# One attention and mixture-of-experts layer: stack copies split over two DMA queues, buffer padding moved, and two engine orders changed

## The chip, the core and the metric

The program runs on one core of one Trainium2 chip. The time is the device time of one execution in microseconds (us). "Engine" means TensorE (PE, the matrix products), VectorE (DVE), ScalarE (ACT), GpSimd (POOL) and SyncE (SP, which here only starts DMA transfers). Each engine runs its own list of instructions strictly in order and waits on semaphores. A wait or a DMA issue that stands in the list holds up everything behind it on that engine.

## What is computed

Sixteen sequences of 128 tokens with 128 features go through one layer. Cut to what matters:

```python
q, k, v = norm(x) @ Wq.T + bq, ctx @ Wk.T + bk, ctx @ Wv.T + bv   # 16 heads of 8 features
s = q @ k.T / sqrt(8) + m[h] * softplus(1000 + |i - j|)           # per head, a slope m[h]
x = x + softmax(s) @ v @ Wo.T + bo
h = norm(x)
c = the two largest of softmax(h @ Wr), zero elsewhere            # 16 experts
x = x + sum_e c[e] * (silu(h @ Wg[e]) * (h @ Wu[e])) @ Wd[e] + shared expert
```

## The kernel before, in words

The 16 sequences are taken as 8 groups of two (`b` is 0 or 1). The work is a software pipeline: `step(f, a, p, q, abuf)` does the feed-forward part of group `f`, the attention of group `a = f + 1`, the query and key projection of group `p = a + 1` and the first normalisation of group `q = p + 1`. Every engine has its own `step`, written out by hand, and that text is the order of its instructions. The calls are: some lines of prologue, `step(None, 0, 1, 2, 0)` (below: step 0), `step(0, 1, 2, 3, 1)` (step 1), a loop of four steps (steps 2 to 5), `step(5, 6, 7, None, 0)` (step 6), `step(6, 7, None, None, 1)` (step 7), and a last stage that does the feed-forward part of group 7.

**Stacks.** The scores need about float32 accuracy, so each query and key value is split into a high and a low float16 part, made by ACT (`qk_high`, L613) and DVE (`qk_low`, L798) in the four slots `t` of `qk_parts`. Four DMAs per group (`stacks`, L211, one for each slot, 128 KB each, 128 partitions to 8) lay them head by head into rows 8t to 8t+7 of `stacks_sb`, which has two buffers. The score products (`scores`, L324 and L327; `scores_T`, L360 to L370) contract over 96 or 98 rows of it. Rows 32 to 95 are never written by the copies and must be zero, and rows 96 and 97 of the key stacks must be one: these are the **pads**. Before, DVE and POOL write them for buffer 0 in the prologue (L1023, L1028, L1034, L1165) and POOL writes those of buffer 1 after step 0 (L1176, L1178, L1180).

**Shift rows.** DVE takes the negated row maxima of the scores (`row_max`, L818), splits them (`max_high`, `max_low`, L824 and L828), PE transposes them (`shift_T`, L336), ACT copies them to `nmT` (L620) and starts a small DMA of 8 KB (`shift_rows`, L630) into rows 96 and 97 of the query stacks. `scores_T(a, b, 0)` waits for that DMA. ACT has had one queue for these, for the router weights (L634) and for some weight loads; SP has had the queue of all else.

**Experts.** PE computes chunk `c` of the hidden layer (`up`, L446 and L451; 9 chunks), ACT takes tanh (L671), DVE multiplies (`gate`, L923; `hidden`, L929). POOL multiplies chunks 0 to 7 in pairs by the router weights (`weigh_experts`, L1139), which were spread by a DMA to `crep` (L218). PE then does `down` (L472) for the chunks, one step late, among the next step's work. In the last stage of the program the weights are spread on PE (`spread`, L564 and L565) and DVE multiplies (`weigh_chunk`, L1043). POOL also computes the inverse deviations (`inverse_deviation2`, L1107 and L1111), which DVE's second normalisation (`norm2`, L870) waits for, and PE's `expert_in_T` (L415) waits for that.

`keep_clock` (L271) issues transposes whose results nobody reads, so that PE has work.

## Time and profile before

| | us |
|---|---|
| median of 3 runs | 289.34 (288.31 to 290.44) |
| the profiled execution | 289.88 |
| span of the profile in it | 288.1 |
| PE busy | 231.9 |
| DVE busy | 185.9 |
| ACT busy | 107.3 |
| POOL busy | 80.9 |

The profile is one execution. Its span leaves out 1.8 us around the instructions. Idle time costs something only where the waiting engine is on the path that sets the end; PE's gaps are therefore what to look for here, and then what each gap waited for.

### The profile page before, as it was taken

The numbers are of one execution on the slowest core, as the hardware profiler recorded it, in microseconds if no ns is written. First come the engines' busy times: TensorE is split into PE (matmuls) and PEld (weight loads), VectorE is DVE, ScalarE is ACT, GpSimd is POOL, SyncE is SP. The second block draws the span as 40 slices with busy tenths as digits, with TensorE's granted clock in tenths as the row PEclk, the third lists the DMA queues.
The fourth block names the chain that finished last, engine by engine and source line by source line (L and its number), as shares of the span: only waits on it lengthen the run. The fifth ranks groups of instructions, "written<-read, shape, count | busy, mean of one in ns | idle before, by whom it ended". The sixth has DMA issues, their size and how long they took to land.

```text
span 288.1 us, 5914 instructions
## 1 busy us (share of the span) xinstructions
PE 231.9 (80%) x1953; PEld 186.5 (65%) x1953; DVE 185.9 (65%) x641; ACT 107.3 (37%) x255; POOL 80.9 (28%) x124
## 2 busy tenths in 40 slices
PE   3634788129887999799979997999799969995896
PEld 3523645027655986688668776877687758765785
DVE  4751823218928883898489758975895587543664
ACT  1151344003462356244614561455235512651320
POOL 3520001793004600451055106410730071017000
PEclk9995578857999999999999999999999988997999
DMA  4244238000450044214511470137023600070000
GB/s 141 83 55 100 45 60 284 0 2 19 57 134 17 23 56 109 59 24 56 135 33 24 54 161 3 37 41 160 4 47 34 167 0 5 3 167 0 0 20 18
DMA packets 16022, 17.54 MB, mean 61 GB/s; under 512 B 1920, under 2 KB 14704, under 8 KB 16000
## 3 DMA queue, kind: packets, MB, share of 16 engines
q1 hardware_dynamic: 14800, 15.83, 25.9%
q10 hardware_dynamic: 1200, 1.43, 1.7%
q8 instruction: 12, 0.20, 0.3%
q14 instruction: 10, 0.08, 0.1%
HBM read 11.77 MB, written 1.16 MB: 45 GB/s over the span
## 4 chain that ended last, share of the span: by engine, by line
PE 39%; issue 27%; POOL 14%; DMA 10%; DVE 5%; ACT 2%; POOLq 1%; SPq 0%; ACTq 0%; DVEq 0%
PE ps_m L472 8%; PE ps_up L446 6%; DMA stacks_sb<-nmT 6%; POOL hid L1139 5%; PE ps_pv L389 4%; PE ps_s L327 3%; PE ps_st L360 3%; DMA stacks_sb<-qk_parts 3%; PE ps_up L451 2%; POOL rstd L1111 2%; PE ps_st L370 2%; PE ps_pv L396 2%; DVE xn L790 1%; PE ps_up L271 1%; DMA x_all<-in_x 1%
## 5 line engine op out<-in xcount | busy, mean ns | idle before, releaser
L472 PE MATMUL ps_m<-wd_sb,hid 128*128 128x128 f32 x288 | 47.2, 294 | 13.3 <-POOL hid L1139 13.3
L818 DVE TENSOR_REDUCE nmax<-ps_s 128x4 f32<-128x512 f32 x64 | 43.4, 682 | 20.7 <-PE ps_s L327 19.8
L923 DVE SCALAR_TENSOR_TENSOR tg<-th,ps_up 128x256 f32<-128x256 f32 x72 | 29.9, 416 | 33.6 <-ACT th L671 33.3
L472 PEld LDWEIGHTS ps_m<-wd_sb,hid 128*128 128x128 f32 x288 | 38.9, 199 | 15.9 <-issue 8.0
L626 ACT ACTIVATE probs<-ps_st 128x512 f32<-128x512 f32 x64 | 38.0, 597 | 29.9 <-PE ps_st L370 25.4
L671 ACT ACTIVATE th<-ps_up 128x256 f32<-128x256 f32 x72 | 27.6, 384 | 35.6 <-PE ps_up L451 35.6
L1139 POOL TENSOR_TENSOR hid<-hid,crep 128x512 f32<-128x512 f32 x28 | 34.7, 1269 | 0.0
L1107 POOL TENSOR_TENSOR ve<-mv,eps_sb 128x1 f32<-128x1 f32 x16 | 3.0, 190 | 96.8 <-DVE mv L863 96.8
L929 DVE TENSOR_TENSOR hid<-tg,ps_up 128x256 f32<-128x256 f32 x72 | 29.6, 411 | 0.7
L327 PE MATMUL ps_s<-stacks_sb 96*128 96x128 f16 x256 | 26.5, 240 | 1.9 <-DVE nmax L818 1.9
L446 PE MATMUL ps_up<-x_hi,wg_hi 128*128 128x256 f32 x72 | 26.9, 374 | 0.5 <-ACT x_hi L652 0.5
L370 PE MATMUL ps_st<-stacks_sb 98*128 98x128 f16 x256 | 25.0, 221 | 0.9 <-ACT probs L626 0.9
L1099 POOL TENSOR_TENSOR ve<-mv,eps_sb 128x2 f32<-128x2 f32 x8 | 1.5, 193 | 85.2 <-DVE mv L782 85.2
L327 PEld LDWEIGHTS ps_s<-stacks_sb 96*128 96x128 f16 x256 | 19.8, 108 | 7.8 <-DVE nmax L818 3.5
L370 PEld LDWEIGHTS ps_st<-stacks_sb 98*128 98x128 f16 x256 | 18.6, 98 | 8.1 <-issue 1.1
L324 PE MATMUL ps_s<-slope_hi,dist 128*128 128x512 f16 x16 | 7.1, 442 | 18.7 <-POOL stacks_sb L1180 10.9
L652 ACT ACTIVATE x_hi<-ps_st 128x256 fp32r<-128x256 f32 x8 | 3.1, 383 | 51.0 <-PE ps_st L415 51.0
L446 PE MATMUL ps_up<-x_hi,wg_lo 128*128 128x256 f32 x72 | 20.4, 284 | 0.0
L446 PE MATMUL ps_up<-x_hi,wu_lo 128*128 128x256 f32 x72 | 20.4, 283 | 0.0
L446 PE MATMUL ps_up<-x_hi,wu_hi 128*128 128x256 f32 x72 | 20.4, 283 | 0.0
L451 PE MATMUL ps_up<-x_lo,wg_hi 128*128 128x256 f32 x72 | 20.4, 283 | 0.0
L451 PE MATMUL ps_up<-x_lo,wu_hi 128*128 128x256 f32 x72 | 20.2, 280 | 0.0
(126 smaller groups left out, 486.2 us busy)
## 6 DMA issues: line engine op xcount, KB each, us to landing
crep<-cw_dram SPq DMA_DIRECT2D x14, 512.0 KB, 6.5
stacks_sb<-qk_parts SPq DMA_DIRECT2D x32, 128.0 KB
out_y<-x_all SPq DMA_DIRECT2D x8, 128.0 KB, 6.3
wg_sb<-in_wgT ACTq DMA_DIRECT2D x1, 576.0 KB, 3.3
wu_sb<-in_wuT ACTq DMA_DIRECT2D x1, 576.0 KB, 3.3
wd_sb<-in_wd SPq DMA_DIRECT2D x1, 576.0 KB, 5.8
x_all<-in_x SPq DMA_DIRECT2D x2, 256.0 KB, 3.4
ctx_all<-in_ctxT SPq DMA_DIRECT2D x2, 256.0 KB, 4.0
```

The costliest lines, as they stand in the source:

```text
L327: last = mm(bank[:, o:o + P], qs[buf][0:ZROWS, h, b * P:(b + 1) * P], ks[buf][0:ZROWS, h, b * P:(b + 1) * P], start=(g > 0), stop=True, sk ...
L370: last = mm(bank[:, o:o + P], ks[buf][:, h, b * P:(b + 1) * P], qs[buf][:, h, b * P:(b + 1) * P], start=first, stop=True, skip_group_check ...
L389: last = mm(ps_pv[32 * c:32 * c + 32, r * 3 * P:(r * 3 + n) * P], v_aug[:, b, r, c, :], probs[:, b, h * P:(h + n) * P], start=True, stop=T ...
L446: mm(ps_up[c % 2][:, k, :], w[:, c, :], x2_hi[:], start=(k == 0 and n == 0), stop=False, skip_group_check=True)
L451: last = mm(ps_up[c % 2][:, k, :], hi[:, c, :], x2_lo[:], start=False, stop=True, skip_group_check=True)
L472: last = mm(ps_dn[:, b * P:(b + 1) * P], hid[:, buf, c, b * P:(b + 1) * P], wd_sb[:, c, :], start=(c == 0 and b == 0), stop=(c == SHARED), ...
L626: fn(probs[:, b, g * HG * P:(g + 1) * HG * P], ps_st[g % 2][:], ACT.Exp).then_inc(exp_sb, 1)
L671: fn(th[:, c % 2, :], ps_up[c % 2][:, 0, :], ACT.Tanh, scale=0.5).then_inc(tanh_sb, 1)
L818: v.tensor_reduce(nmax[:, b, HG * g:HG * g + HG], ps_s[g % 2][:].rearrange("p (h j) -> p h j", h=HG), AX_X, ALU.max, negate=True).then_inc ...
L923: v.scalar_tensor_tensor(out=tg[:, c % 2, :], in0=th[:, c % 2, :], scalar=1.0, in1=ps_up[c % 2][:, 0, :], op0=ALU.add, op1=ALU.mult).then_ ...
L929: v.tensor_tensor(hid[:, buf, c, :], tg[:, c % 2, :], ps_up[c % 2][:, 1, :], ALU.mult).then_inc(hid_sb, 1)
L1139: g.tensor_tensor(h2, h2, c2, ALU.mult).then_inc(hc_sb, 1)
```

## The change

- **Pads.** DVE zeroes all 98 rows of half of buffer 0, ACT the other half and the ones of buffer 0, both at the start. ACT writes zeros and ones of buffer 1 in the prologue, after its slope tables. POOL writes no pads.
- **Prologue on DVE.** The scaling of the query weights stands ahead of the first normalisation.
- **Query and key parts.** On ACT `qk_high` comes ahead of `x2_high`; on DVE the two `qk_low` come between the first three `row_max` of a step.
- **Stack slots.** Slots 0 and 1 are issued by SP, slots 2 and 3 by ACT (`mixed_stacks`), behind `tanh(f, 1)` and ahead of the copy and the DMA of the first shift rows.
- **POOL.** Pair 0 of the experts of group `f` is weighed at the end of step `f`, between the two inverse deviations, in place of the start of the next.
- **Last stage.** `expert_in_T` comes behind two `down` chunks in place of four, the other `down` of group 6 follow, and all `down` of group 7 come at the end. The DVE order is adapted.

```diff
@@ sync
-                for t in range(4):
+                for t in range(2):
                     if t == 1:
                         sp.wait_ge(qklo_sb, 2 * p + 2)
                     sp.dma_start(stacks_sb[DH * t:DH * (t + 1), buf]..., qk_parts[:, t]...).then_inc(s_stack, 16)
@@ scalar
+            def mixed_stacks(p, buf):
+                if not (at_start(p) or (isinstance(p, int) and p == 1)):
+                    act.wait_ge(st_mm, 2 * NHG * (p - 1))
+                if at_start(p):
+                    act.wait_ge(dve_pads, 1)
+                elif isinstance(p, int) and p == 1:
+                    act.wait_ge(act_pads, 3)
+                act.wait_ge(qklo_sb, 2 * p + 2)
+                for t in range(2, 4):
+                    act.dma_start(stacks_sb[DH * t:DH * (t + 1), buf]..., qk_parts[:, t]...).then_inc(s_stack, 16)
+                if ps: qk_high(p)
                 if fs: x2_high(f)
-                if ps: qk_high(p)
                 if fs:
                     tanh(f, 0)
                     tanh(f, 1)
+                if ps: mixed_stacks(p, 1 - abuf)
...
+            act.wait_ge(zero_sb, 2)
+            fill(stacks_sb[:, 0, H // 2:], zero)
+            act.wait_ge(act_pads, 1)
+            act.wait_ge(dve_pads, 1)
+            fill(ks[0][ZROWS:AROWS], ones16)
             x_T(0)
...
             qk_high(0)
+            mixed_stacks(0, 0)
...
+            fill(stacks_sb[:, 1], zero)
+            act.wait_ge(act_pads, 3)
+            fill(ks[1][ZROWS:AROWS], ones16)
             act.wait_ge(s_stack, 64)
             act.dma_start(wu_sb[:], wuT).then_inc(s_wu, 16)
@@ vector
                     row_max(a, 0, 1)
-                    row_max(a, 0, 2)
+                if ps: qk_low(p, 0)
+                if as_: row_max(a, 0, 2)
+                if ps: qk_low(p, 1)
@@ gpsimd
-                    for pair in range(PAIRS):
+                    for pair in range(1, PAIRS):
                         weigh_experts(f - 1, pair, abuf)
...
                     inverse_deviation2(a, 0)
+                    if f is not None:
+                        weigh_experts(f, 0, 1 - abuf)
                     inverse_deviation2(a, 1)
...
-            g.memset(stacks_sb[SROWS:2 * SROWS, 1].bitcast(F32), 0.0).then_inc(second_pads, 1)
-            g.memset(stacks_sb[2 * SROWS:ZROWS, 1].bitcast(F32), 0.0).then_inc(second_pads, 1)
-            g.memset(ks[1][ZROWS:AROWS].bitcast(F32), two_ones).then_inc(second_pads, 1)
@@ tensor, last stage
-            down(f - 1, (0, 1, 2, 3), 1 - last, f)
+            down(f - 1, (0, 1), 1 - last, f)
             expert_in_T(f)
+            down(f - 1, (2,), 1 - last)
...
-            down(f, range(2, NCH), last, weighted_sb=hw_sb)
+            down(f, range(NCH), last, weighted_sb=hw_sb)
```

ACT at the start of step 1, before. L604 is the transposed input, L652 the high part of the experts' input, L613 the high parts of queries and keys, L671 tanh, L620 and L630 the shift rows' copy and DMA:

```order
L604 ACTIVATE xnT<-ps_st 128x256
L652 ACTIVATE x_hi<-ps_st 128x256
L613 ACTIVATE qk_parts<-ps_st,bqk_sb 128x2x256 x2
L671 ACTIVATE th<-ps_up 128x256 x2
L620 ACTIVATE nmT<-ps_pv 32x128
L630 DMA stacks_sb<-nmT 2x16x128
L671 ACTIVATE th<-ps_up 128x256
```

The same place with the change (L653 is a stack slot, L620 and L627 stand for the parts of queries and keys and for the shift rows' copy, L637 for their DMA):

```order
L611 ACTIVATE xnT<-ps_st 128x256
L620 ACTIVATE qk_parts<-ps_st,bqk_sb 128x2x256 x2
L672 ACTIVATE x_hi<-ps_st 128x256
L691 ACTIVATE th<-ps_up 128x256 x2
L653 DMA stacks_sb<-qk_parts 8x16x512 x2
L627 ACTIVATE nmT<-ps_pv 32x128
L637 DMA stacks_sb<-nmT 2x16x128
L691 ACTIVATE th<-ps_up 128x256
```

The two stack slots now stand between tanh and the shift rows, and the parts come ahead of the experts' input.

DVE at the start of step 1, before (L870 is norm2, L877 the low part of the experts' input, L798 the low parts of queries and keys):

```order
L870 TENSOR_SCALAR x2n<-x_all,mv,rstd 128x128
L818 TENSOR_REDUCE nmax<-ps_s 128x4 x2
L877 TENSOR_TENSOR x_lo<-ps_st,x_hi 128x256
L818 TENSOR_REDUCE nmax<-ps_s 128x4
L824 CAST nsplit<-nmax 128x16
L923 SCALAR_TENSOR_TENSOR tg<-th,ps_up 128x256
L828 TENSOR_TENSOR nsplit<-nmax,nsplit 128x16
L929 TENSOR_TENSOR hid<-tg,ps_up 128x256
L798 SCALAR_TENSOR_TENSOR qk_parts<-ps_st,bqk_sb,qk_parts 128x2x256
L818 TENSOR_REDUCE nmax<-ps_s 128x4
L798 SCALAR_TENSOR_TENSOR qk_parts<-ps_st,bqk_sb,qk_parts 128x2x256
```

The same place with the change:

```order
L904 TENSOR_SCALAR x2n<-x_all,mv,rstd 128x128
L852 TENSOR_REDUCE nmax<-ps_s 128x4
L832 SCALAR_TENSOR_TENSOR qk_parts<-ps_st,bqk_sb,qk_parts 128x2x256
L852 TENSOR_REDUCE nmax<-ps_s 128x4
L832 SCALAR_TENSOR_TENSOR qk_parts<-ps_st,bqk_sb,qk_parts 128x2x256
L911 TENSOR_TENSOR x_lo<-ps_st,x_hi 128x256
L852 TENSOR_REDUCE nmax<-ps_s 128x4
L858 CAST nsplit<-nmax 128x16
L957 SCALAR_TENSOR_TENSOR tg<-th,ps_up 128x256
L862 TENSOR_TENSOR nsplit<-nmax,nsplit 128x16
L963 TENSOR_TENSOR hid<-tg,ps_up 128x256
```

The two low parts moved from behind the first `hidden` to ahead of the experts' low part.

POOL in the second half of step 1, before (L1099 and L1103 are the inverse deviations of the first normalisation, L1107 and L1111 those of the second):

```order
L1132 COPY ctx_g<-ctx_all 128x256
L1099 TENSOR_TENSOR ve<-mv,eps_sb 128x2
L1103 TENSOR_TENSOR rstd<-ve,neg_half 128x2
L1107 TENSOR_TENSOR ve<-mv,eps_sb 128x1
L1111 TENSOR_TENSOR rstd<-ve,neg_half 128x1
L1107 TENSOR_TENSOR ve<-mv,eps_sb 128x1
L1111 TENSOR_TENSOR rstd<-ve,neg_half 128x1
```

The same place with the change:

```order
L1168 COPY ctx_g<-ctx_all 128x256
L1135 TENSOR_TENSOR ve<-mv,eps_sb 128x2
L1139 TENSOR_TENSOR rstd<-ve,neg_half 128x2
L1143 TENSOR_TENSOR ve<-mv,eps_sb 128x1
L1147 TENSOR_TENSOR rstd<-ve,neg_half 128x1
L1175 TENSOR_TENSOR hid<-hid,crep 128x512
L1143 TENSOR_TENSOR ve<-mv,eps_sb 128x1
L1147 TENSOR_TENSOR rstd<-ve,neg_half 128x1
```

One pair's multiply (L1175) now stands between the two inverse deviations of the second normalisation.

## Rows read from the trace of the kernel before

**Rows 1.** Waits, longest first: engine, line, what released it: us, times, longest.

```profile
PE ps_m L472 <- POOL hid L1139: 13.3, 7, 3.1
...
PE ps_s L324 <- POOL stacks_sb L1180: 10.9, 1, 10.9
```

**Rows 2.** Timeline 0 to 38: start, us, engine, line, operation, count, idle before, releaser.

```profile
6.29 3.68 DVE L790 TENSOR_SCALAR xn<-x_all,mv,rstd 128x128 f32<-128x128 f32 x2 [1.16 <-POOL rstd L1103]
6.31 3.50 POOL L1165 MEMSET stacks_sb<- 32x4096 f32 x1
...
14.66 3.38 SPq L211 DMA_DIRECT2D stacks_sb<-qk_parts  x4
...
25.59 0.61 PE L324 MATMUL ps_s<-slope_hi,dist 128*128 128x512 f16 x1 [7.42 <-DMA stacks_sb<-qk_parts]
...
28.90 1.26 ACT L613 ACTIVATE qk_parts<-ps_st,bqk_sb 128x512 f16<-128x512 f32 x2 [1.69 <-PE ps_st L293]
...
37.00 0.63 PE L360 MATMUL ps_st<-slope_hi,dist 128*128 128x512 f16 x1
```

**Rows 3.** A group by form on ACT: busy us, mean ns of one, idle before.

```profile
L739 ACT ACTIVATE wg_hi<-wg_sb 128x1152 fp32r<-128x1152 f32 x1 | 1.2, 1163 | 6.3 <-DMA stacks_sb<-qk_parts 6.3
```

**Rows 4.** Timeline of step 0, second shift rows on ACT, and SP's next transfer behind them.

```profile
39.06 0.63 ACTq L630 DMA_DIRECT2D stacks_sb<-nmT  x1
...
41.22 0.34 SPq L227 DMA_DIRECT2D x_all<-in_x  x1
```

**Rows 5.** Timeline of PE in step 4, a step of the loop.

```profile
149.95 0.71 PE L472 MATMUL ps_m<-wd_sb,hid 128*128 128x128 f32 x4 [1.39 <-POOL hid L1139]
...
159.27 0.38 PE L360 MATMUL ps_st<-slope_hi,dist 128*128 128x512 f16 x1
...
160.63 0.23 PE L336 MATMUL ps_pv<-ident,nsplit 128*32 128x128 f16 x1
...
165.31 0.38 PE L360 MATMUL ps_st<-slope_hi,dist 128*128 128x512 f16 x1 [0.40 <-DMA stacks_sb<-nmT]
```

**Rows 6.** Timeline of DVE in the same step.

```profile
149.06 0.92 DVE L870 TENSOR_SCALAR x2n<-x_all,mv,rstd 128x128 f32 x1
...
152.24 0.42 DVE L877 TENSOR_TENSOR x_lo<-ps_st,x_hi 128x256 fp32r<-128x256 f32 x1 [0.62 <-ACT x_hi L652]
...
155.97 0.73 DVE L798 SCALAR_TENSOR_TENSOR qk_parts<-ps_st,bqk_sb,qk_parts 128x512 f16<-128x512 f32 x1
...
174.49 0.34 DVE L870 TENSOR_SCALAR x2n<-x_all,mv,rstd 128x128 f32 x1 [0.19 <-POOL rstd L1111]
```

**Rows 7.** Timeline of ACT and SP in the same step (q: the engine's DMA issues).

```profile
154.48 0.38 ACT L671 ACTIVATE th<-ps_up 128x256 f32<-128x256 f32 x1 [0.84 <-PE ps_up L451]
...
155.25 0.67 ACTq L630 DMA_DIRECT2D stacks_sb<-nmT  x1
...
161.19 0.63 ACTq L630 DMA_DIRECT2D stacks_sb<-nmT  x1
...
153.29 5.42 SPq L211 DMA_DIRECT2D stacks_sb<-qk_parts  x4
```

**Rows 8.** Busy time by microsecond, same step: last columns clock, DMA share, GB/s.

```profile
158.00:159.00 1.00, 1.00 (x10) 0.98 (x9) 1.00 (x4) 0.12 (x1) 0.00 (x0) 1.00 0.51 126
159.00:160.00 1.00, 1.00 (x11) 0.75 (x11) 0.97 (x3) 0.42 (x2) 0.00 (x0) 1.00 0.57 54
...
163.00:164.00 1.00, 1.00 (x15) 0.95 (x12) 0.74 (x5) 0.82 (x2) 0.08 (x1) 1.00 0.36 29
```

**Rows 9.** Timeline of PE, starts of step 7 and of the last stage.

```profile
234.34 0.68 PE L472 MATMUL ps_m<-wd_sb,hid 128*128 128x128 f32 x4 [2.48 <-POOL hid L1139]
...
262.84 3.47 PE L472 MATMUL ps_m<-wd_sb,hid 128*128 128x128 f32 x16 [3.15 <-POOL hid L1139]
```

**Rows 10.** Timeline of DVE at the start of the last stage and the end.

```profile
261.51 1.27 DVE L870 TENSOR_SCALAR x2n<-x_all,mv,rstd 128x128 f32<-128x128 f32 x1 [0.63 <-POOL rstd L1111]
...
285.30 0.42 DVE L934 TENSOR_TENSOR x_all<-ps_m,x_all 128x256 f32<-128x256 f32 x1 [1.29 <-PE ps_m L472]
```

More of the change, by code:

```diff
@@ L314, in scores @@
                         pe.wait_ge(act_setup, 1)
-                        pe.wait_ge(own, 8)
-                        pe.wait_ge(stack_pads, 2)
+                        pe.wait_ge(own, 7)
+                        pe.wait_ge(dve_pads, 1)
+                        pe.wait_ge(act_pads, 1)
                     elif isinstance(a, int) and a == 1:
-                        pe.wait_ge(second_pads, 3)
+                        pe.wait_ge(act_pads, 4)
                 elif b == 0 and g == 1:
@@ L572, in _ @@
             up(f, 1)
+            down(f - 1, (3,), 1 - last)
+            up(f, 2)
             down(f - 1, (4,), 1 - last)
-            up(f, 2)
+            up(f, 3)
             down(f - 1, (5,), 1 - last)
-            up(f, 3)
+            up(f, 4)
             down(f - 1, (6,), 1 - last)
             weights_T(f, None)
-            up(f, 4)
+            up(f, 5)
             down(f - 1, (7,), 1 - last)
@@ L584, in _ @@
             spread(0, 1)
-            up(f, 5)
+            up(f, 6)
             down(f - 1, (8,), 1 - last)
             spread(2, 3)
-            up(f, 6)
+            up(f, 7)
             spread(4, 5)
-            down(f, (0,), last, weighted_sb=hw_sb)
-            up(f, 7)
+            up(f, 8)
             spread(6, 7)
-            down(f, (1,), last, weighted_sb=hw_sb)
-            up(f, 8)
-            down(f, range(2, NCH), last, weighted_sb=hw_sb)
+            down(f, range(NCH), last, weighted_sb=hw_sb)
         @block.scalar
@@ L717, in step, with fill @@
                 if fs: tanh(f, 8)
+            def fill(tile, column):
+                words = tile.bitcast(F32)
+                fn(words, bass.AP(column, 0, [[1, words.shape[0]]] + [[0, n] for n in words.shape[1:]]), ACT.Copy).then_inc(act_pads, 1)
             nc.scalar.preload_act_table(ACT.Exp)
-            act.wait_ge(s_x, 16)
+            act.wait_ge(zero_sb, 2)
[3 more added lines that the diff above has]
+            fill(ks[0][ZROWS:AROWS], ones16)
             x_T(0)
@@ L751, in _ @@
             tanh(f, 3)
+            tanh(f, 4)
             act.wait_ge(cwT_mm, f + 1)
             fn(cwT_hi[:], ps_cwT, ACT.Copy).then_inc(cwT_sb, 1)
-            for c in range(4, NCH):
+            for c in range(5, NCH):
                 tanh(f, c)
@@ L959, in step @@
                 if fs: hidden(f, 0, 1 - abuf)
-                if ps: qk_low(p, 0)
                 if as_: row_max(a, 1, 0)
-                if ps: qk_low(p, 1)
                 if fs: gate(f, 1)
@@ L1020, in step @@
                     norm2_mean(a, 1)
-            v.memset(stacks_sb[2 * SROWS:ZROWS, 0, 0:H // 2].bitcast(F32), 0.0).then_inc(stack_pads, 1)
-            step(None, None, None, 0, 0)
+            v.memset(zero[:], 0.0).then_inc(zero_sb, 1)
+            v.memset(ones16[:], two_ones).then_inc(zero_sb, 1)
+            v.memset(stacks_sb[:, 0, 0:H // 2].bitcast(F32), 0.0).then_inc(dve_pads, 1)
+            norm1_stats(0)
+            norm1_mean(0)
             dve.wait_ge(s_wqkvo, 32)
@@ L1027, in _ @@
             v.tensor_scalar(bqk_sb[:, 0:1], bqk_sb[:, 0:1], q_scale, None, ALU.mult).then_inc(dve_setup, 1)
-            v.memset(stacks_sb[2 * SROWS:ZROWS, 0, H // 2:].bitcast(F32), 0.0).then_inc(stack_pads, 1)
+            norm1(0)
             norm1_stats(1)
@@ L1033, in _ @@
             norm1(1)
-            v.memset(ks[0][ZROWS:AROWS].bitcast(F32), two_ones).then_inc(stack_pads, 1)
             values(0)
@@ L1045, in _ @@
             gate(f - 1, 8)
+            hidden(f - 1, 8, 1 - last)
             norm2(f, 1)
-            hidden(f - 1, 8, 1 - last)
             x2_low(f)
@@ L1064, in _ @@
             hidden(f, 3, last)
+            gate(f, 4)
+            hidden(f, 4, last)
             dve.wait_ge(cwT_sb, f + 1)
             v.tensor_tensor(cwT_lo[:], ps_cwT, cwT_hi[:].bitcast(F32), ALU.subtract).then_inc(cwTlo_sb, 1)
-            gate(f, 4)
-            hidden(f, 4, last)
+            gate(f, 5)
+            hidden(f, 5, last)
             weigh_chunk(0)
-            gate(f, 5)
-            residual2(f - 1)
-            hidden(f, 5, last)
             weigh_chunk(1)
             gate(f, 6)
+            residual2(f - 1)
+            hidden(f, 6, last)
             weigh_chunk(2)
-            hidden(f, 6, last)
             weigh_chunk(3)
             gate(f, 7)
+            hidden(f, 7, last)
             weigh_chunk(4)
-            hidden(f, 7, last)
             weigh_chunk(5)
             gate(f, 8)
+            hidden(f, 8, last)
             weigh_chunk(6)
-            hidden(f, 8, last)
             weigh_chunk(7)
@@ L1164, in _ @@
             pool.wait_ge(rstd1_sb, 1)
-            g.memset(stacks_sb[SROWS:2 * SROWS, 0].bitcast(F32), 0.0).then_inc(own, 1)
-            pool.wait_ge(own, 7)
             copy_ctx(0)
@@ L1185, in _ @@
             run_steps(pool, step)
-            for pair in range(PAIRS):
+            for pair in range(1, PAIRS):
                 weigh_experts(NG - 2, pair, (NG - 2) % 2)
```

19 lines of the change are left out of this document (12 added, 7 removed).

## The prediction

> **What bounds the kernel now.** I read the list of waits first, because a long wait of PE points at a place. Two stand out. PE waited once for 10.9 us for POOL's pads of buffer 1, and 7 times, 13.3 us in all, for POOL's first expert pair [rows 1]. The timeline of the prologue shows why the start is slow: two normalisation multiplies took 3.68 us together while POOL's 3.50 us memset ran beside them, and the first stacks came 10.93 us after SP began to issue them (14.66 to 25.59) [rows 2]. In a loop step PE's own rows tell how much of the 13.3 us is to be had. PE waited 1.39 us for POOL at 149.95, then had work nearly without a gap to the first `scores_T` at 159.27, the second `shift_T` at 160.63 and `scores_T` of the second sequence at 165.31, which waited 0.40 us for the second shift rows [rows 5]. But DVE in the same stretch had a gap of only 0.62 us [rows 6], and PE follows DVE's row maxima there. So DVE is the near bound of the first half of a step, and at most some 0.6 us of the 1.39 us can come back by moving POOL alone. At the starts of step 7 and of the last stage PE waits 2.48 and 3.15 us [rows 9].
>
> **Part 1, pads and prologue.** POOL's three memsets leave, so PE's wait of 10.9 us goes [rows 1]. What is late next is not POOL: PE had been done with step 0 at 51.9 (62.81 less 10.91), and the normalisation chain of step 0 was finished some 1.5 us later, for which PE has 1.5 us of scores and projections to do first. I take 10.9 us.
>
> DVE's multiplies, without the memset beside them, should take 0.7 instead of 3.68 us: one such multiply took 0.34 us beside an idle POOL [rows 6]. PE's warm-up transposes end at 7.2, so PE starts about 2.8 us earlier. The stacks are then issued from 11.8 and 13.3 instead of 14.66 and 16.1. With all four slots served as before they are complete 9.5 us after the second of these, at 22.8, against 25.59.
>
> Against this stand ACT's fills. 1152 elements took 1163 ns [rows 3], so 4096 take 3.6 to 4.1 us and 2048 about 1.9 us. The first two (3.9 us) lie in ACT's idle time before 10 us and cost nothing. The pair of buffer 1 (5.5 us) stands behind the slope tables, which end near 18.9, so ACT is busy until 24.4, and with the 1.4 us of weight copies behind it until 26. `qk_high` of group 1 began at 28.90 before [rows 2], and can now begin at 26.1 at the earliest, even if the stacks are there sooner. `qk_low` now stands ahead of DVE's third row maximum, so step 0 hangs on this. Adding DVE's own times puts the end of its row maxima at 33.0 (34.9 before) and PE's `scores_T` at 35.2 by engines alone, against 37.00 before [rows 2]: 1.8 us earlier. The first shift rows, however, now stand in ACT's queue behind slots 2 and 3, which are issued from 29.5. They land at 35.6 if the two queues run side by side, at 37.8 if slots 1 to 3 share one rate. So step 0 moves by between -1.4 and +0.8 us. I take -0.4, between them. Prologue and step 0 together: -10.9 - 0.4 = **-11.3 us** (-10.1 to -12.7). Step 1 has fewer PE chunks and waited 1.38 us for its second shift rows; there the loss of part 2 and this wait cancel.
>
> **Part 2, slots 2 and 3 on ACT.** This is the part that can cost. First the speed of a slot. A slot that is alone moves its 128 KB in one microsecond (126 GB/s). Slots 2 and 3, queued behind it, move at 54 GB/s and are at it until about 163.6 [rows 8], so each takes 2.25 us. The share of busy DMA time is about a half in either case. From issue (156.8 for slot 1) a first slot is done after 2.2 us, a second after 4.45 us. Shift rows: the second ones were issued at 161.19, while slots were moving, and PE got them at 165.31, 4.1 us later [rows 5, 7]. In step 0 a set issued at 39.06 had landed when SP went on at 41.22, 2.15 us later [rows 4].
>
> With the change, in the times of that step: ACT's `tanh(f, 1)` is dispatched at about 154.7 (154.48 before [rows 7], PE being 0.2 us later, as below). Each slot then takes the queue 0.65 us to issue, as SP's four took 5.42 us with a wait inside [rows 7]; the copy of the shift rows comes 1.3 us later, and their DMA is issued at 156.35 in place of 155.25. In the same queue it stands behind two slots that are complete 4.45 us after 154.75, at 159.2. It moves after them and lands 1.1 to 1.6 us after its data, near 160.9. PE needed it at 159.27 [rows 5]. It had 4.0 us of cover before, and has none now.
>
> What comes back: the second shift rows no longer meet moving slots and land in some 2.2 us, so the 0.40 us wait goes [rows 5], and DVE, ahead while PE stands, no longer holds `shift_T` back, 0.25 us. Net: 1.6 - 0.65 = +0.95 us in a step. The steps that have both a stack and a full load are 2 to 6, five of them.
>
> The Trainium skill bears on this twice. Its page "DMA: Bandwidth & Descriptors" says under "Why a DMA increments its semaphore by 16 and not by 1" that a DMA uses as many engines as divide the slowest dimension of both sides, from the lowest number up: 8 for a slot with 8 destination partitions, 2 for the shift rows, so these two share rings. The half share in the rows agrees. Under "Issuing engines are not separate DMA queues" it says that issuing from several engines saves only the issue time. That speaks against splitting; by it step 0 is 1.2 us worse than I took.
>
> **Part 3, POOL order and DVE parts.** Down chunk 0 no longer waits for POOL. In a loop step PE spends that time waiting elsewhere: `qk_low` twice (0.7 us each [rows 6]) now stands ahead of the experts' low part, which moves from 152.24 to about 152.9, so PE ends its first `up` chunk 0.4 us later than before, and the DVE gap of 0.62 us closes. By the first `scores_T` PE would be only 0.2 us ahead, and part 2 takes that. New at the end of a step is POOL's 1.26 us multiply beside DVE. A DVE multiply took 0.92 us at 149.06 beside POOL and 0.34 us at 174.49 without [rows 6]; about 0.25 us of this gets onto the chain to the next row maximum. It needs `crep`, whose data ended near 173.0 in this step, to have landed by 174.45; it probably has. So +0.15 to +0.25 us in a step, and part 2 and 3 together are **+1.1 us in each of five steps, +5.5 us**. Bounds for one step: -0.2, if the slots on ACT go at the rate of lone ones (shift rows land at 159.5), and +2.8, if they hold the shift rows until 162.5.
>
> **Part 4, step 7 and last stage.** No stacks are copied here. In step 7 PE's 2.48 us wait goes [rows 9]; what is late next is `norm2`, which ends at 234.3, against a transpose at 235.6 before, and from 236 to 239 the granted clock was 0.5 (1.2 GHz), after the idle time. I take -2.2 (between -1.0, with the clock as before, and -3.0). In the last stage `expert_in_T` need not wait for four pairs, only for `norm2` at 262.8 (261.51 + 1.27 [rows 10]) in place of 266.1. PE's work is the same in sum and saturates PE from 273 on; its end at 285.30 [rows 10] comes earlier by the idle time saved, 3.3 us less one `down` chunk (0.45) and less what a low clock costs again. I take -2.5 (-1.5 to -3). Together **-4.7 us**.
>
> **Sum.** 289.88 for the profiled execution - 11.3 + 5.5 - 4.7 = 279.4. It was 0.5 us above the median of the three runs, so by the median 278.9, rounded to 279.
>
> **Rivals.** (A) The shift rows keep their cover: slots on ACT go like lone ones or the small DMA is served between them. For: PE's trace shows a first slot done in one microsecond of data. Against: the second of a pair never did. -0.2 in a step gives 289.3 - 11.3 - 1.0 - 4.7 = 272.3. (B) The shift rows wait longer, +2.8 in a step: 289.3 - 11.3 + 14 - 4.7 = 287.3; half way, 283.5. For: the 4.1 us of the set that met the slots in another queue; a shared queue can only be harder. (C) Slower than before: the same wait, from the point where it costs 3.2 us net in a step, that is where the shift rows land at 163 or later, 6.7 us after their issue, because each slot on ACT then takes above 3.2 us. At +4 us in a step it is 289.3 - 16.0 + 20 = 293.3. Against: no slot took more than 2.3 us. (D) POOL's moved pair waits for `crep` and holds up the second inverse deviation, as POOL does nothing behind a waiting instruction. If it lands 1 us later than I read, 0.7 us in six steps is added: 283. (E) The pads' gain is not had, because ACT's fills hold step 0: with `qk_high` 3 us later than I took, 282.
>
> **How the numbers follow.** Forecast, 276 to 282: 0.50. (A), 270 to 276: 0.22. (B), (D) and (E), 282 to 286.4: 0.14. Within 1%, 286.4 to 292.2, about what a measurement here can tell from no change (the upper end of B): 0.07. (C) and worse: 0.07. Range 270.5 to 286.4, which leaves out some 0.15, and it takes in both ends of parts 1 and 2. Faster 0.86, same 0.07, slower 0.07.
>
> **What would show each step.** Part 1: no PE wait for POOL near 50; the first normalisation multiplies near 0.7 us; `scores_T` of step 0 at 35 to 38. Part 2: a PE wait of 1 to 2 us for the shift rows' DMA ahead of the first `scores_T` of every loop step, and none ahead of the second sequence's. Part 3: PE's wait for the first expert pair gone, a loop step of 29.3 us in place of 28.25. Part 4: a shorter wait for POOL and a first `up` of the last stage 3 us sooner in its stage. The prediction is wrong if the loop step is not longer than before, or if it is longer than 31 us.

## The result, and the profile after

The changed kernel took **295.82 us** (median; 293.68 to 296.28) against 288.82 us (287.98 to 290.44) for the kernel before: ratio 1.022, 95% interval 1.015 to 1.029. It is slower by 2.2%, where I had forecast 279. Its profiled execution took 296.10 us with a span of 294.3 us; the one of before took 289.88 us. The ratios leave out executions in a slower state that any kernel can fall into, so a ratio can differ from that of the medians beside it (most in the experiment with 281.26 us, whose profiled execution was also in that state).

The start of each step, read from PE's first scores in both timelines, splits the difference of 6.2 us between the two profiled executions:

| stretch | before, us | after, us | difference | predicted |
|---|---|---|---|---|
| up to the scores of step 1 | 62.81 | 51.05 | -11.8 | -11.3 |
| step 1 | 27.46 | 33.28 | +5.8 | 0 |
| steps 2 to 6 | 28.08, 28.46, 28.04, 28.28, 27.90 | 31.97, 31.76, 30.33, 30.38, 30.35 | +14.0 | +5.5 |
| step 7 and last stage, to the end of the span | 57.07 | 55.18 | -1.9 | -4.7 |

So the start gained what was forecast, and the steps gave back more than all of it. The list of waits of the changed kernel, longest first (engine, line, what released it: us, times, longest):

```profile
PE ps_st L367 <- DMA stacks_sb<-nmT: 13.7, 7, 2.9
PE ps_st L422 <- DVE x2n L904: 8.3, 8, 3.2
...
PE ps_s L334 <- DVE nmax L852: 5.2, 13, 0.6
PE ps_up L458 <- DVE x_lo L911: 4.6, 6, 0.9
```

The waits for POOL of [rows 1] are gone, both of them. First now is the wait of `scores_T` for the shift rows; before it was 3.1 us in 5 waits, all for the rows of the second sequence. Step 4 shows where it comes from. PE's timeline (start, us, operation, idle time ahead and what ended it), beside [rows 5]:

```profile
148.06 0.39 PE L331 MATMUL ps_s<-slope_hi,dist 128*128 128x512 f16 x1
...
149.65 0.61 PE L479 MATMUL ps_m<-wd_sb,hid 128*128 128x128 f32 x4
...
154.97 0.38 PE L458 MATMUL ps_up<-x_lo,wg_hi 128*128 128x256 f32 x1 [0.88 <-DVE x_lo L911]
...
163.29 0.39 PE L367 MATMUL ps_st<-slope_hi,dist 128*128 128x512 f16 x1 [2.02 <-DMA stacks_sb<-nmT]
...
178.39 0.38 PE L331 MATMUL ps_s<-slope_hi,dist 128*128 128x512 f16 x1
```

From the step's first scores to the first `scores_T` it took 15.23 us, against 12.46 before (146.81 to 159.27), and from there to the next step 15.10 against 15.58. All of this step's loss lies ahead of `scores_T`. DVE in the same stretch, beside [rows 6]:

```profile
147.50 1.28 DVE L904 TENSOR_SCALAR x2n<-x_all,mv,rstd 128x128 f32 x1 [0.19 <-POOL rstd L1147]
...
152.59 0.73 DVE L832 SCALAR_TENSOR_TENSOR qk_parts<-ps_st,bqk_sb,qk_parts 128x512 f16<-128x512 f32 x1
...
153.85 0.73 DVE L832 SCALAR_TENSOR_TENSOR qk_parts<-ps_st,bqk_sb,qk_parts 128x512 f16<-128x512 f32 x1
154.51 0.41 DVE L911 TENSOR_TENSOR x_lo<-ps_st,x_hi 128x256 fp32r<-128x256 f32 x1
```

and ACT, beside [rows 7]:

```profile
156.73 0.38 ACT L691 ACTIVATE th<-ps_up 128x256 f32<-128x256 f32 x1 [0.84 <-PE ps_up L458]
156.89 1.38 ACTq L653 DMA_DIRECT2D stacks_sb<-qk_parts  x2
158.46 0.27 ACT L627 ACTIVATE nmT<-ps_pv 32x128 f16<-32x128 f16 x1 [1.35 <-issue]
158.76 0.68 ACTq L637 DMA_DIRECT2D stacks_sb<-nmT  x1
```

The shift rows are issued 10.70 us into the step, 8.44 before. Of these 2.26 us, 1.35 us is ACT issuing the two slots; the rest came from DVE, where `norm2` (L904) took 1.28 us beside POOL's moved pair and `x_lo` (L911) stands behind both `qk_low` (L832). From their issue to `scores_T` the rows then took 4.5 us, as forecast. Before, PE came to `scores_T` 4.0 us after the issue and found the rows there.

Step 1 lost most. DVE, POOL and PE at its start, three rows of the changed kernel's timeline:

```profile
53.03 3.26 DVE L904 TENSOR_SCALAR x2n<-x_all,mv,rstd 128x128 f32<-128x128 f32 x1 [0.37 <-POOL rstd L1147]
53.09 3.13 POOL L1213 TENSOR_SCALAR wd_sb<-wd_sb 128x1152 f32<-128x1152 f32 x1
56.35 0.69 PE L422 MATMUL ps_st<-ident,x2n 128*128 128x128 f32 x2 [3.23 <-DVE x2n L904]
```

POOL's scaling of `wd`, which stood behind its pads before, now runs beside `norm2` of group 0, and PE waits 3.23 us. Of busy time and clock (the last three columns are granted clock, DMA share and GB/s) the next 11 us show:

```profile
57.00:68.00 11.00, 10.50 (x53) 8.77 (x50) 8.07 (x22) 2.11 (x7) 0.65 (x3) 0.50 0.23 37
```

PE is busy but at half clock, 1.2 GHz.

### The profile page after: what moved, and what is told of

The parts are those of the page before. It is cut to its first block, busy times and chain, and to the rows that moved or that the text cites. A ratio compares the mean times of both kernels' runs of the same rounds, so it can differ in the third digit from the quotient of the medians.

```text
span 294.3 us, 5927 instructions
## 1 busy us (share of the span) xinstructions
PE 238.4 (81%) x1953; PEld 191.0 (65%) x1953; DVE 184.2 (63%) x641; ACT 116.5 (40%) x259; POOL 68.7 (23%) x120
## 4 chain that ended last, share of the span: by engine, by line
PE 42%; issue 21%; DMA 11%; ACT 8%; DVE 7%; POOL 6%; ACTq 4%; POOLq 0%; DVEq 0%; SPq 0%
DMA stacks_sb<-nmT 10%; PE ps_up L453 7%; PE ps_m L479 5%; PE ps_st L367 5%; PE ps_pv L396 4%; PE ps_up L458 4%; POOL hid L1175 4%; PE ps_st L377 4%; ACTq L653 3%; DVE nmax L852 2%; ACT qk_parts L620 2%; PE ps_pv L403 2%; DVE qk_parts L832 2%; PE ps_m L416 2%; ACT probs L633 1%
## 5 line engine op out<-in xcount | busy, mean ns | idle before, releaser
L852 DVE TENSOR_REDUCE nmax<-ps_s 128x4 f32<-128x512 f32 x64 | 43.3, 681 | 10.5 <-PE ps_s L334 9.9
L1175 POOL TENSOR_TENSOR hid<-hid,crep 128x512 f32<-128x512 f32 x28 | 35.0, 1271 | 0.5 <-DMA crep<-cw_dram 0.5
L453 PE MATMUL ps_up<-x_hi,wg_hi 128*128 128x256 f32 x72 | 27.9, 388 | 0.0
L377 PE MATMUL ps_st<-stacks_sb 98*128 98x128 f16 x256 | 26.9, 232 | 0.0
L377 PEld LDWEIGHTS ps_st<-stacks_sb 98*128 98x128 f16 x256 | 20.4, 106 | 8.5 <-issue 3.2
L458 PE MATMUL ps_up<-x_lo,wg_hi 128*128 128x256 f32 x72 | 21.8, 302 | 4.6 <-DVE x_lo L911 4.6
L367 PE MATMUL ps_st<-slope_hi,dist 128*128 128x512 f16 (+1 forms) x32 | 13.1, 409 | 13.9 <-DMA stacks_sb<-nmT 13.7
L904 DVE TENSOR_SCALAR x2n<-x_all,mv,rstd 128x128 f32<-128x128 f32 (+1 forms) x16 | 20.1, 1255 | 2.4 <-POOL rstd L1147 2.0
L453 PE MATMUL ps_up<-x_hi,wg_lo 128*128 128x256 f32 x72 | 21.2, 295 | 0.0
L453 PE MATMUL ps_up<-x_hi,wu_hi 128*128 128x256 f32 x72 | 21.1, 293 | 0.0
L453 PE MATMUL ps_up<-x_hi,wu_lo 128*128 128x256 f32 x72 | 21.1, 293 | 0.0
L458 PE MATMUL ps_up<-x_lo,wu_hi 128*128 128x256 f32 x72 | 21.0, 292 | 0.0
```

Of the source, the lines that this page charges most:

```text
L367: mm(bank[:, 0:n_split * P], dist16[:], part[:, h0:h0 + n_split, :], start=first, stop=False, skip_group_check=True)
L377: last = mm(bank[:, o:o + P], ks[buf][:, h, b * P:(b + 1) * P], qs[buf][:, h, b * P:(b + 1) * P], start=first, stop=True, skip_group_check ...
L453: mm(ps_up[c % 2][:, k, :], w[:, c, :], x2_hi[:], start=(k == 0 and n == 0), stop=False, skip_group_check=True)
L458: last = mm(ps_up[c % 2][:, k, :], hi[:, c, :], x2_lo[:], start=False, stop=True, skip_group_check=True)
L852: v.tensor_reduce(nmax[:, b, HG * g:HG * g + HG], ps_s[g % 2][:].rearrange("p (h j) -> p h j", h=HG), AX_X, ALU.max, negate=True).then_inc ...
L1175: g.tensor_tensor(h2, h2, c2, ALU.mult).then_inc(hc_sb, 1)
```

## Experiments

Each edit is against the changed kernel unless another is named. The intervals are those of the ratio to the kernel before, measured on the same chip. Three theories stood at first: (1) the slots on ACT's queue hold up the shift rows; (2) the loss is made on DVE; (3) step 1 loses by the scaling of `wd`.

**All slots back on SyncE.**

```
SP:  -for t in range(2):      +for t in range(4):
ACT: -if ps: mixed_stacks(p, 1 - abuf)
```

> The changed kernel with slots 2 and 3 back behind slots 0 and 1 on SyncE's queue; everything else of the change stays. Theory 1 (the two slot issues on ScalarE, 1.38 us ahead of the shift rows, and the slots' place ahead of the rows in ScalarE's queue, are the main loss): in each of steps 2 to 6 the shift rows are issued about 1.3 us earlier, the time from the first scores to scores_T(a,0), 15.2 us in step 4 of the changed kernel, falls to about 13.3, the wait of 2.0 us there is gone, and the time is 284 to 288 us. Theory 2 (the loss is made on VectorE at the step's start, by POOL's multiply beside norm2 and by qk_low ahead of x_lo, and the wait for the rows only hides it): the rows' wait shrinks but others take its place, 15.2 falls to 14.7 at most, and the time is 292 to 295 us.

293.77 us, ratio 1.019 (1.014 to 1.024): the same as the changed kernel within the intervals, and the time that theory 2 expected. My first theory fell in this form. The rows of step 4 (its first scores are at 145.22) say why:

```profile
151.21 1.98 SPq L217 DMA_DIRECT2D stacks_sb<-qk_parts  x3
...
154.11 0.66 ACTq L637 DMA_DIRECT2D stacks_sb<-nmT  x1
...
159.67 0.54 PE L367 MATMUL ps_st<-slope_hi,dist 128*128 128x512 f16 x1 [1.79 <-DMA stacks_sb<-nmT]
```

The same kernel by microseconds (granted clock, DMA share and GB/s last):

```profile
156.00:157.00 1.00, 1.00 (x12) 0.99 (x12) 0.58 (x3) 0.50 (x2) 0.00 (x0) 1.00 0.53 53
157.00:158.00 1.00, 0.88 (x8) 0.68 (x6) 1.00 (x4) 0.38 (x1) 0.00 (x0) 1.00 0.57 66
158.00:159.00 1.00, 0.00 (x0) 0.00 (x0) 1.00 (x10) 0.00 (x0) 0.00 (x0) 1.00 0.08 5
```

The rows are issued 8.9 us into the step (9.5 on the mean of steps 2 to 6; 10.7 in the changed kernel, 8.5 before), but take 5.56 us to PE instead of the changed kernel's 4.5. What ACT saved by not issuing slots, 1.2 us, went again in the longer transfer: `scores_T` starts 15.2 us into these steps on the mean, 15.3 in the changed kernel. Nothing stands ahead of them on their own queue. Ahead of them on the other queue are slots 1, 2 and 3, since the early `qk_low` releases these at 151.21; their bytes move until about 158.1, and PE has the rows 1.6 us after that. In the changed kernel the same reading gives 1.3 us (traffic at a share of 0.40 up to 162, 0.01 behind it, `scores_T` at 163.29). So the rows reach PE 1.3 to 1.6 us after the last byte of the slots issued ahead of them, on whichever queue. Theory 1 was restated so: what counts is the slot bytes issued ahead of the rows.

**Shift rows first, two queues kept.**

```
ACT:  shift_rows(a, 0, abuf)
     +if ps: mixed_stacks(p, 1 - abuf)     (was ahead of shift_copy)
```

> The changed kernel with mixed_stacks moved behind shift_rows(a, 0) on ScalarE: still two queues, but the shift rows of the first block go ahead of the two slots. Theory 1 in its narrow form (it is the order on ScalarE alone): as good as the kernel with all slots on SyncE, 284 to 288 us, since the slots are wanted only in the next step. Rival (any slot traffic on a second queue slows the rows, whatever the order): the rows still take over 4 us from issue to scores_T and the time stays at 290 us or more. Theory 2: 292 to 295 us.

281.26 us, ratio 0.967 (0.961 to 0.973), 15.9 us less than the changed kernel by the ratios, and better than the 284 to 288 expected. No wait for the rows is left in the list of waits; in step 4 they went at 145.97, slots 2 and 3 at 146.85, and `scores_T` started without a wait at 149.57. Slots that follow 0.9 us behind, then, do not delay the rows as slots ahead of them do. The edit also takes ACT's two slot issues (1.34 us) out of the rows' way.

```profile
145.97 0.70 ACTq L637 DMA_DIRECT2D stacks_sb<-nmT  x1
146.85 1.34 ACTq L653 DMA_DIRECT2D stacks_sb<-qk_parts  x2
```

**Pair 0 back at the step's start.**

```
POOL: -for pair in range(1, PAIRS):   +for pair in range(PAIRS):
      -if f is not None: weigh_experts(f, 0, 1 - abuf)
```

> The changed kernel with POOL's pair 0 back at the start of the next step; slots stay on two queues. Theory 2: norm2(a,0) goes back from 1.28 to about 0.34 us, the rows are issued 0.5 us earlier in each step and the time is 292 us or less. Theory 1: the rows still wait for the two slots, so at most 0.5 us per step comes back, and down(0)'s wait for POOL (1.4 us in step 4 of the kernel before, 2.5 and 3.2 us in step 7 and the last stage) returns: 295 to 299 us.

297.66 us, ratio 1.030 (1.023 to 1.036). In step 4 `norm2` of block 0 is back at 0.35 us, `down` waits 1.30 us for POOL again, and the wait for the rows is 2.04 us as in the changed kernel. This is within the 295 to 299 us that theory 1 expected; the intervals of the two kernels overlap. On the mean of steps 2 to 6 the rows were issued 0.45 us earlier than in the changed kernel, which is about half of DVE's share of the delay there, and `scores_T` came 0.5 us earlier. What this gained was lost behind `scores_T`: in four of these steps the granted clock averaged 0.90 there (in two of the changed kernel's), and the one step at full clock took 29.90 us against 30.38.

**Pads and prologue alone** (the kernel before with this part of the change).

> The kernel before with only the pads and the prologue's order of the change (slots all on SyncE, loop steps and last stage as before). The sum as predicted for this part: 277 to 279 us (11 us below the kernel before). Theory 3 (part of this gain is lost again in step 1, where norm2 now runs beside POOL's scaling of wd, 3.26 us against 1.50, and TensorE's clock falls to half after the wait of 3.23 us for x2n): step 1 takes about 31 us instead of 27.5 and the time is 281 to 285 us.

276.55 us, ratio 0.960 (0.955 to 0.964): 11.8 us gained by the medians, 13.8 between the two profiled executions. The first scores of step 1 came at 46.53, 16.3 us earlier than before and 4.5 earlier than in the changed kernel, whose step 0 is 4.4 us longer (29.3 against 24.9). Step 1 took 29.1 us here, not 27.5, so 1.7 us of the gain is lost there, less than theory 3 said; the rest of the 5.8 us needs the other parts.

**qk_low late again, all slots on SyncE.** Beside the edit of the first experiment:

```
DVE:  row_max(a, 0, 1)
     -if ps: qk_low(p, 0)
      row_max(a, 0, 2)
     -if ps: qk_low(p, 1)
      ...
      hidden(f, 0, 1 - abuf)
     +if ps: qk_low(p, 0)
      row_max(a, 1, 0)
     +if ps: qk_low(p, 1)
```

> The changed kernel with all slots on SyncE and with qk_low back at its late place on VectorE (behind hidden(f,0)); pads, pair 0, qk_high first and last stage stay changed. Theory 1, as it stands after the first four runs (the shift rows wait for the bytes of all slots that were issued ahead of them, on either queue; qk_low's early place puts slots 1 to 3 ahead): slots 1 to 3 fall behind the rows again, the waits of 1.9 us for the rows in steps 2 to 6 are gone, x_lo comes 0.9 us earlier, and the time is 272 to 278 us, 16 to 21 below the kernel with all slots on SyncE and qk_low early (293.8). Rival (a slow row transfer has to do with ScalarE's issue or with the multiply beside norm2, not with qk_low's place): 288 us or more.

272.62 us, ratio 0.943 (0.939 to 0.948). This is at the low end of what theory 1 expected. With all slots on SyncE the place of two instructions of 0.73 us on DVE is worth 21 us. Step 4 (first scores 132.34) beside the first experiment: the rows go 8.3 us into it, and `scores_T` starts at 144.56 without a wait, 12.2 us into it.

```profile
135.50 8.49 SPq L217 DMA_DIRECT2D stacks_sb<-qk_parts  x4
...
140.65 0.67 ACTq L637 DMA_DIRECT2D stacks_sb<-nmT  x1
```

```profile
142.00:143.00 1.00, 1.00 (x10) 0.83 (x9) 1.00 (x3) 0.38 (x1) 0.00 (x0) 1.00 0.03 6
143.00:144.00 1.00, 1.00 (x10) 0.90 (x10) 1.00 (x5) 0.00 (x0) 0.00 (x0) 1.00 0.32 72
```

SP holds four slots in 8.49 us because it waits for `qk_low` behind slot 0. By microseconds (DMA share and GB/s at the end of the row) almost nothing moves from 138 to 143, and the rows pass ahead of slots 1 to 3.

**All slots behind the landed first rows.** The kernel of the first experiment with one wait more:

```
SP: +if not at_start(p): sp.wait_ge(s_nm[0], 16 * p)
```

> The changed kernel with all slots on SyncE and one more wait there: the slots of the next group are issued only when the first block's shift rows of this group have landed; qk_low stays early. Theory 1: no slot byte is ahead of the rows, they need 2 to 2.5 us from issue, no wait for them is left and the time is at or below the kernel that issues the rows ahead of slots 2 and 3 (281.3): 277 to 281 us. Rival (slots 0 and 1 must go early or they are late for the next step): a wait for stacks at the step's start, above 283 us.

317.70 us, ratio 1.100 (1.095 to 1.105), far from what I expected. I had thought of the first rows alone. In step 4 they are free, but the second ones are now behind all four slots:

```profile
168.83 2.73 SPq L219 DMA_DIRECT2D stacks_sb<-qk_parts  x4
...
172.20 0.63 ACTq L639 DMA_DIRECT2D stacks_sb<-nmT  x1
...
179.63 0.38 PE L369 MATMUL ps_st<-slope_hi,dist 128*128 128x512 f16 x1 [3.74 <-DMA stacks_sb<-nmT]
```

7.4 us from issue to PE with four slots ahead, 5.6 with three (SyncE alone), 4.5 with two (the changed kernel): the miss is the clearest reading of the same rule. Counted are the slots ahead whose bytes had still to move when the rows were issued.

**The rest of the change, cut up.** One kernel keeps pads, pair 0 and last stage (slots on SyncE, `qk_low` late, `qk_high` behind `x2_high`); the other keeps pads and pair 0.

> The changed kernel without its part on the stack and the q/k parts: slots all on SyncE, qk_low late, qk_high behind x2_high; it keeps pads, pair 0 on POOL at the step's end, and the last stage. Against pads alone (276.6) theory 1 has nothing for or against pair 0; from the rows of the changed kernel: no down waits for POOL any more (13.3 us in 7 waits before), x2n waits 0.3 to 0.6 us in each step, the last stage saves about 2 us: 271 to 275 us. Theory 2 (the multiply beside norm2 costs about what the waits for POOL gave): 275 to 278 us.

> Pads and pair 0 of the change alone; last stage, slots and q/k parts as in the kernel before. Tells pair 0 (against pads alone, 276.6) from the last stage (against the kernel that has it as well). Pair 0 predicted by the waits it removes in steps 2 to 7: 0 to 0.6 us a step, so 273 to 277 us; if norm2 beside the multiply costs more than the waits gave, 277 to 280 us. The last stage is predicted at 2 to 2.5 us by my term.

273.16 us (ratio 0.943, 0.939 to 0.947) and 276.81 us (0.955, 0.948 to 0.961), both as expected. Against pads alone (0.960) pair 0 moves nothing that these intervals tell; the last stage brings 3.4 us by the ratios, give or take 2, and `qk_high` first, which the kernel with 272.62 us has as well, nothing. At the start of the last stage PE waited for

```profile
248.36 3.75 PE L479 MATMUL ps_m<-wd_sb,hid 128*128 128x128 f32 x16 [3.15 <-POOL hid L1159]
```

```profile
247.82 0.69 PE L422 MATMUL ps_st<-ident,x2n 128*128 128x128 f32 x2 [1.60 <-DVE x2n L889]
```

the first with pads alone, the second with pads, pair 0 and last stage: the wait of 3.15 us for POOL became one of 1.60 us for `norm2`.

**qk_low late, two queues, rows first.** The second experiment with the DVE edit of the fifth.

> The changed kernel with qk_low late and with slots 2 and 3 on ScalarE behind the first shift rows: two queues, and no slot but slot 0 ahead of the rows. Against all slots on SyncE with qk_low late (272.6) it tells what the second queue does by itself: theory 1 says nothing for the first rows; the two slots, waiting for the late qk_low, hold ScalarE about 1.4 us plus up to 2 us ahead of tanh(2) and sit ahead of the second rows: 273 to 279 us. Rival (the second queue helps, as the change intends): under 272 us.

272.64 us, ratio 0.942 (0.935 to 0.948), equal to all slots on SyncE and between what the two expectations gave. The second queue by itself does nothing that can be told, for or against. The second experiment, which differs only in `qk_low`'s place, is 7.4 us slower by the ratios. In its list of waits 4.6 us in 6 waits for `x_lo` stand, and none here. But the steps of the two profiled executions (282.41 and 273.17 us) show most of the difference where TensorE's clock was low. In brackets is the mean granted clock ahead of the first `scores_T` and behind it:

| step | `qk_low` early, us | `qk_low` late, us |
|---|---|---|
| 1 | 31.28 (0.66, 0.92) | 29.27 (0.87, 1.00) |
| 2 | 28.25 (1.00, 1.00) | 27.94 (1.00, 1.00) |
| 3 | 29.93 (0.88, 1.00) | 28.31 (1.00, 1.00) |
| 4 | 27.82 (1.00, 1.00) | 27.42 (1.00, 1.00) |
| 5 | 28.29 (1.00, 1.00) | 28.06 (1.00, 1.00) |
| 6 | 32.57 (0.71, 1.00) | 28.62 (0.88, 1.00) |

At full clock, DVE's own share of the loss is 0.2 to 0.4 us in a step once the rows are out of it; such steps are as short as the kernel's before (27.90 to 28.46). The lower clock is not that one execution's alone: the two executions on which the ratio rests averaged 0.92 and 0.93, the four with the late `qk_low` 0.95 to 0.96. Whether the early `qk_low` brings it on was not tested.

**The kernel before with qk_low early and nothing else.**

> The kernel before with one edit: qk_low at its early place on VectorE (behind row_max(a,0,1) and row_max(a,0,2)). Theory 1: slots 1 to 3 are issued ahead of the first shift rows, the rows take 5.5 us instead of 4.0 from issue, and each of steps 1 to 6 becomes 2 to 4 us longer, as between the changed kernels with qk_low early and late (21 us): 300 to 312 us. Rival (it needs the multiply beside norm2 as well, or the waits for POOL in this kernel cover it): 290 to 296 us.

322.14 us, ratio 1.110 (1.102 to 1.117), more than I expected. A third price comes in here. ACT still makes `qk_high` behind `x2_high`, so DVE stands at the early `qk_low` and `x_lo` behind it is late:

```profile
171.07 0.75 DVE L798 SCALAR_TENSOR_TENSOR qk_parts<-ps_st,bqk_sb,qk_parts 128x512 f16<-128x512 f32 x1 [2.50 <-ACT qk_parts L613]
...
173.46 0.38 PE L451 MATMUL ps_up<-x_lo,wg_hi 128*128 128x256 f32 x1 [2.83 <-DVE x_lo L877]
...
181.87 0.39 PE L360 MATMUL ps_st<-slope_hi,dist 128*128 128x512 f16 x1 [2.10 <-DMA stacks_sb<-nmT]
```

This suggests that with an early `qk_low`, `qk_high` has to go first as it does in the changed kernel, though no pair of runs set that order apart; with a late one it is worth nothing, as the kernels with 273.16 and 272.62 us show.

**Slots 2 and 3 behind the second rows** (on the kernel with 272.62 us), without and with POOL's scaling of `wd` held.

```
SP:   +if t == 2 and not at_start(p): sp.wait_ge(s_nm[1], 16 * p)
POOL: +pool.wait_ge(x2n_sb, 2)        (ahead of the scaling; second kernel only)
```

> The kernel with all slots on SyncE and qk_low late (272.6), with one more wait on SyncE: slots 2 and 3 go only when the second block's shift rows have landed. Theory 1: only slot 1 and what is left of slot 0 can be ahead of the second rows, so the wait of 0.4 to 0.5 us in each of steps 2 to 6 and of 1.5 us in step 1 goes; the slots, issued about 19 us into the step, still land before the next step's scores: 268.5 to 271.5 us. Rival (those short waits are covered by something else, exp or x2n): 272 to 273 us. If the slots come too late for the next step: a wait for stacks at its start, above 274 us.

> The kernel that sends slots 2 and 3 behind the second rows, with POOL's scaling of wd held until norm2 has written both blocks of group 0. Theory 3 (norm2(0,1) takes 3.26 us because POOL scales wd beside it, and the wait of 3.2 us for x2n lets TensorE's clock fall in step 1): norm2 takes 0.3 to 0.9 us, the wait falls under 1 us and the time is 2.5 to 5 us below the kernel without this: 265 to 268 us. Rival (the wait is covered by what follows, or the scaling now lies beside something as costly): less than 1 us.

297.45 us (292.56 to 301.55, too scattered for a ratio) and 291.87 us (ratio 1.008, 1.003 to 1.012). Both expectations failed: no new wait for the stacks came, but another. The next victim of the slots is the 16 KB write of `cwT`, from which `crep` is made. Step 3 of the second kernel:

```profile
126.05 1.28 SPq L219 DMA_DIRECT2D stacks_sb<-qk_parts  x2
...
127.44 0.33 ACTq L643 DMA_DIRECT2D cw_dram<-cwT  x1
...
132.81 1.53 SPq L226 DMA_DIRECT2D crep<-cw_dram  x2
...
140.27 1.26 POOL L1162 TENSOR_TENSOR hid<-hid,crep 128x512 f32<-128x512 f32 x1 [3.32 <-DMA crep<-cw_dram]
```

The write lands in 5.1 us (median) instead of 1.4, `crep` goes 5.4 us after it, and POOL waits 3.32 us with pair 0, with the second inverse deviation of `norm2` behind it. PE's waits for POOL's product come back, 14.4 us in 6 waits. That is the mechanism of my rival (D). In the changed kernel POOL waited for `crep` once, 0.5 us.

**POOL's scaling of wd held**, on the kernel with 272.62 us and on the changed kernel.

> The kernel with all slots on SyncE and qk_low late (272.6), with POOL's scaling of wd held until norm2 has written both blocks of group 0. Theory 3: in step 1 the wait of 3.23 us for x2n falls under 1 us, and step 1 goes from 29.3 to 26 to 27 us: 268.5 to 270.5 us. Rival (the scaling then lies beside add_bo's and copy_ctx's turn on POOL and makes something else late, or the wait was covered): 272 to 273 us.

> The changed kernel itself with POOL's scaling of wd held in the same way. Theory 3 for the changed kernel's step 1 (33.3 us against 27.5 before, the largest loss of a single step): 3 us of it are the wait for x2n and its low clock, the rest is what qk_low's place and the rows cost in every step: 290.5 to 293.5 us. Rival (the clock falls in step 1 for another reason, so only the wait's own 2.3 us can come back, or none since the rows' wait takes it up): 293.5 to 296 us.

**270.16 us**, ratio 0.936 (0.934 to 0.939), and 293.07 us, ratio 1.015 (1.011 to 1.018), both as theory 3 expected. The first is the best kernel of this study, 6.4% under the kernel before. Its step 1 takes 26.35 us instead of 29.26:

```profile
49.31 0.35 DVE L889 TENSOR_SCALAR x2n<-x_all,mv,rstd 128x128 f32<-128x128 f32 x1 [0.37 <-POOL rstd L1132]
...
49.72 0.44 PE L422 MATMUL ps_st<-ident,x2n 128*128 128x128 f32 x2 [0.32 <-DVE x2n L889]
...
49.86 3.13 POOL L1199 TENSOR_SCALAR wd_sb<-wd_sb 128x1152 f32<-128x1152 f32 x1 [0.58 <-DVE x2n L889]
```

```profile
47.00:58.00 11.00, 9.39 (x73) 7.39 (x73) 10.21 (x27) 3.46 (x9) 5.25 (x7) 0.96 0.13 30
```

With 0.32 us of waiting in place of 3.23, the clock of this stretch is 0.96 (0.84 without the hold). In the changed kernel step 1 falls from 33.28 to 30.35 us, the same 2.9 us: theory 3 holds for half of this step's 5.8 us. The other half was not set apart; a wait of 0.85 us for the rows and a low clock (0.67 ahead of `scores_T`, 0.88 behind it) are left in it.

## Why the prediction was wrong

The forecast was -10.5 us and the profiled executions moved by +6.2. Of the 16.7 us between them, 5.8 are step 1, 8.5 the steps 2 to 6 and 2.8 part 4; part 1 gives 0.5 back.

**Part 1** (-11.3) had the number right: -11.8 at the scores of step 1. PE's wait of 10.9 us went, as forecast. The scores of step 0 came at 21.74 (22.8 forecast). For step 0 two errors cancelled. I had put its `scores_T` at 35.2 by engines alone, and with pads and prologue alone it came at 33.02. In the changed kernel it came at 37.09, between my bounds of 35.6 and 37.8 for the rows: DVE's early `qk_low` waited 2.25 us for ACT's `qk_high`, and PE then 2.87 us for the rows. With the rows first it came at 33.99. Beside this I had set the Trainium skill ("DMA: Bandwidth & Descriptors", "Issuing engines are not separate DMA queues"), by which issuing from several engines saves only issue time. In step 0 the time lay nearer to the bound that I drew from it. Both pairs of kernels that differ in which engine issues slots 2 and 3 agree with it (1.022 and 1.019; 0.942 and 0.943).

**Step 1 as neutral** failed: +5.8 us. I had written that POOL was not what is late next, and had looked only at the normalisation chain. The memsets that left had kept POOL's scaling of `wd` away from `norm2`. That the two would get in each other's way could have been read from the rows: `norm2` took 0.92 us beside POOL's 1.26 us multiply and 0.34 without [rows 6]. Beside the 3.13 us scaling it took 3.26. Without that overlap step 1 is 2.9 us shorter; the rest is open.

**Parts 2 and 3, +1.1 us in a step**, failed in size and in cause: +2.1 to +2.5 us in steps 4 to 6, +3.9 and +3.3 in steps 2 and 3, which at 31.97 and 31.76 us are also longer than the 31 us that I had named as a sign of being wrong. Three terms were wrong.
- Mis-sized: the rows' issue, forecast 1.1 us later than before, came 2.3 us later. The slots' share (1.3 us) was right. What I gave DVE, 0.2 us for `qk_low` ahead and 0.15 to 0.25 us for the multiply beside `norm2`, was about 0.9 us together, half of it by the multiply. The rows had no cover left by my own working, so PE's wait of 2.0 us came as forecast, but 1.1 us later in the step. With the rows out of the way the early `qk_low` costs 0.2 to 0.4 us in a step at full clock.
- Misplaced: I blamed ACT's queue. With all slots on SyncE the loss stays, because the early `qk_low` sends slots 1 to 3 ahead of the rows there. I never asked what the early `qk_low` does to SP, where slot 1 waits for it, though SP's two groups of slots stood in [rows 7]. The order of rows and slots, with ACT's two issues, is worth 15.9 us.
- Left out: the clock. After the 2 us wait in step 2 it was 0.57 of full speed from 100 to 104, and in step 3 it averaged 0.79 from 131 to 139; in steps 4 to 6, with the same wait, it stayed at 1.00. That fits the 1.4 to 1.6 us by which steps 2 and 3 are longer than the others. No run set the clock apart, so this share is read and not tested.

**Part 4** (-4.7) gave -1.9. Step 7's wait of 2.48 us for POOL [rows 9] went, but four shorter waits, for the residual, a row maximum, `norm2` and a row maximum, took its place (0.28, 0.42, 0.74 and 0.49 us): from the first scores to those of the second sequence 7.45 us, 7.41 before. So the -2.2 there was nothing. I had named `norm2` as late next and still booked the gain. The last stage gave 1.9 us in the profiled execution and 3.4 us by the cut-up kernels, around my 2.5.

**The rivals.** What happened is the outcome of (C), a step with more than 3 us of loss in some steps, but not its condition: no slot took above 3.2 us, and the rows landed in 4.5 us as forecast. What I had not counted was made ahead of their issue. (B) had the right size per step, +2.8, for the wrong reason and by luck, as the clock is in that mean. (D) was a real mechanism with another trigger. (A) did not come about. Nor did (E): ACT's fills took 1.9 and 3.6 us as forecast, and `qk_high` of group 1 began at 25.05 (26.1 forecast).

## What to carry to other kernels

Before moving an instruction earlier, list what it releases on other engines, their DMAs above all, and which small, urgent transfer then stands behind these; a split over two queues changed nothing in that here. Send the small transfer that the next product waits for first, and large ones in the gap behind it, and check each of the small ones of the step, not the first alone. When work leaves an engine, look at what moves up behind it and what that now runs beside.
